# A two-layer conditional attention kernel: the opening in another order, GpSimd's long subtractions in four parts, both probability-value groups side by side

## What is computed

```python
# layer 0: linear attention, 8 heads
q = softmax((xn @ Wq + bq) per head);  k = softmax((xn @ Wk + bk + mask) over the rows)
att = einsum('bnhd,bnhl->bhdl', k, v);  y = einsum('bnhd,bhdl->bnhl', q, att)
# layer 1: softmax attention, 16 heads
att = softmax(einsum('bnhl,bmhl->bnmh', q, k) + mask, axis=2);  y = einsum('bnmh,bmhl->bnhl', att, v)
# both
scale, shift = split(silu(cond) @ W_emb + b_emb)
x = x + silu(ln(y) * (1 + scale) + shift) @ W_out + b_out
```

## Time and profile before

| | before |
|---|---|
| median of 3 runs | 2180.84 us (2180.38 to 2180.98) |
| the profiled execution | 2180.41 us |
| its span, first to last instruction | 2178.6 us |
| TensorE matmuls busy | 2140.4 us, 98% |
| VectorE busy | 1400.7 us, 64% |
| ScalarE busy | 910.7 us, 42% |
| GpSimd busy | 563.9 us, 26% |
| mean granted TensorE clock | 0.995 |

### The profile page before, as it was taken

How to read it: one execution, slowest core, us unless ns; L and a number is a source line. 1 busy time by engine, 2 the same in 40 slices (tenths; PEclk the granted TensorE clock), 3 DMA queues, 4 the chain that set the end, 5 groups by cost and what they waited for, 6 DMA issues and landing times.

```text
span 2178.6 us, 53551 instructions
## 1 busy us (share of the span) xinstructions
PE 2140.4 (98%) x20955; PEld 1859.2 (85%) x20955; DVE 1400.7 (64%) x2986; ACT 910.7 (42%) x2088; POOL 563.9 (26%) x890
## 2 busy tenths in 40 slices
PE   6999999999999999999999999999999999999997
PEld 4888888888888888877888888888888888888886
DVE  6777777777777777766564656565555555555554
ACT  3333333333333333442444444444444444445444
POOL 4233333233333233323222212121212121212120
PEclk9999999999999999999999999999999999999999
DMA  6211000111000111103000000000101010101000
GB/s 207 107 39 39 29 34 34 39 39 39 29 34 34 39 39 39 38 21 117 20 29 29 29 29 30 28 36 22 39 19 39 19 39 19 39 19 39 19 31 21
DMA packets 52165, 86.47 MB, mean 40 GB/s; under 512 B 5667, under 2 KB 14565, under 8 KB 52134
## 3 DMA queue, kind: packets, MB, share of 16 engines
q1 hardware_dynamic: 52118, 86.03, 11.2%
q10 hardware_dynamic: 16, 0.00, 0.0%
HBM read 52.32 MB, written 33.69 MB: 39 GB/s over the span
## 4 chain that ended last, share of the span: by engine, by line
PE 94%; DVE 2%; ACT 1%; issue 1%; DMA 1%; SPq 0%; POOL 0%; DVEq 0%; ACTq 0%
PE bank L537 14%; PE bank L538 13%; PE bank L539 13%; PE bank L546 9%; PE bank L547 8%; PE bank L548 8%; PE bank L1650 5%; PE bank L1676 3%; PE bank L1105 3%; PE bank L1682 3%; PE bank L1693 2%; PE bank L1093 2%; PE bank L1006 1%; PE bank L1616 1%; PE bank L1030 1%; PE bank L1034 1%
## 5 line engine op out<-in xcount | busy, mean ns | idle before, releaser
L546 PE MATMUL bank<-xT_hi,w_hi 128*128 128x256 f32 x1536 | 449.1, 292 | 1.1 <-DVE top L1322 1.1
L547 PE MATMUL bank<-xT_lo,w_hi 128*128 128x256 f32 x1536 | 441.1, 287 | 0.0
L548 PE MATMUL bank<-xT_hi,w_lo 128*128 128x256 f32 x1536 | 437.6, 285 | 0.0
L537 PE MATMUL bank<-w_hi,xT_hi 128*128 128x512 f32 x768 | 316.2, 412 | 4.4 <-DVE bias_all L401 4.4
L546 PEld LDWEIGHTS bank<-xT_hi,w_hi 128*128 128x128 f32 x1536 | 291.3, 190 | 19.9 <-issue 8.9
L539 PE MATMUL bank<-w_lo,xT_hi 128*128 128x512 f32 x768 | 307.1, 400 | 0.0
L538 PE MATMUL bank<-w_hi,xT_lo 128*128 128x512 f32 x768 | 304.0, 396 | 0.0
L547 PEld LDWEIGHTS bank<-xT_lo,w_hi 128*128 128x128 f32 x1536 | 291.8, 190 | 1.5 <-issue 0.2
L548 PEld LDWEIGHTS bank<-xT_hi,w_lo 128*128 128x128 f32 x1536 | 292.4, 190 | 0.0
L537 PE MATMUL bank<-w_hi,h_hi 128*128 128x512 f32 x512 | 217.6, 425 | 5.9 <-DVE h_lo L1364 3.7
L926 ACT ACTIVATE heads<-bank,k_neg 128x128 f32<-128x128 f32 x256 | 70.0, 372 | 358.3 <-DVE k_neg L791 358.3
(11 more groups left out here) (210 smaller groups left out, 4053.6 us busy)
## 6 DMA issues: line engine op xcount, KB each, us to landing
xr<-in_x SPq DMA_DIRECT2D x32, 512.0 KB, 3.4
x_between_layers<-ends SPq DMA_DIRECT2D x64, 256.0 KB, 2.0
xr<-x_between_layers SPq DMA_DIRECT2D x32, 512.0 KB, 3.6
out<-ends SPq DMA_DIRECT2D x64, 256.0 KB, 2.0
store<-in_L_cond_W_emb SPq DMA_DIRECT2D x4, 1024.0 KB, 11.4
mask_rows<-mask_parts SPq DMA_DIRECT2D x128, 2.0 KB
heads<-in_L_cond_emb_w SPq DMA_DIRECT2D x2, 1024.0 KB, 7.2
store<-in_L_cond_emb_w SPq DMA_DIRECT2D x2, 1024.0 KB, 11.5
```

The costliest lines, as they stand in the source:

```text
L537: yield nc.tensor.matmul(bank[:, :], a_hi[:, c, b, :], w_hi[:, m, c, :], start=(c == 0), stop=False)
L546: yield nc.tensor.matmul(dst, w_hi[:, m, c, fs], a_hi[:, c], start=(first and c == 0), stop=False)
L547: yield nc.tensor.matmul(dst, w_hi[:, m, c, fs], a_lo[:, c], start=False, stop=False)
L548: yield nc.tensor.matmul(dst, w_lo[:, m, c, fs], a_hi[:, c], start=False, stop=(last and c == C - 1))
```

## The change

It has three parts.

In the opening, the conditioning vector is loaded behind the key weights, and its tanh, product and transposes move back on all engines, to behind the first half of the projections. The key bias is loaded with the first small loads. ScalarE issues its four mask DMAs ahead of the high part of the key weights, reports each of the four parts of a high part, and copies the key sums behind the turned rows. VectorE normalises the first pair ahead of the low part of the key weights and makes the low part of the value weights behind the query bias. TensorE projects feature groups 0 and 2 of the first keys ahead of the query sums and adds their bias later. GpSimd makes the low part of the output weights in four parts and adds the value bias later.

At the hand-over, GpSimd's `low` goes in four parts, with one report at the end.

In layer 1's loop, `mixed` of both sequences stand side by side, both `turned` are woven into the last two query projections, and VectorE and ScalarE follow: `end_outputs` of both ahead of `end_norm`, `copy_yT` of both ahead of the second half of the queries.

The core of the diff:

```diff
@@ -211,9 +211,9 @@
...
-    loads = [(cond, T["cond_2048"]),
-             (mask_in[:, 0, :], T["mask_BxSx1_fk1"].rearrange("b s o -> b (s o)")),
-             (mask_in[:, 1, :], T["mask_BxS_ff1"])]
+    loads = [(mask_in[:, 0, :], T["mask_BxSx1_fk1"].rearrange("b s o -> b (s o)")),
+             (mask_in[:, 1, :], T["mask_BxS_ff1"]),
+             (m.key_row, T["L0_cond_bk"].rearrange("(o d) -> o d", o=1))]
...
@@ -230,7 +230,8 @@
...
-        sp.dma_start(m.key_row, T["L0_cond_bk"].rearrange("(o d) -> o d", o=1)).then_inc(small_in3, 16)
+            if n == K:
+                sp.dma_start(cond, T["cond_2048"]).then_inc(cond_in, 16)
         for k, name in ((BQ, "L0_cond_bq"), (BV, "L0_cond_bv"), (BO, "L0_cond_b_out")):
             sp.dma_start(m.bias_all[:, k, :], row_everywhere(name)).then_inc(small_in3, 16)
...
@@ -277,21 +278,23 @@
...
-        pool.wait_ge(s["split_hi"], 4)
-        nc.gpsimd.tensor_tensor(m.w_lo[:, O], raw[O], f32(m.w_hi[:, O]), ALU.subtract).then_inc(s["out_lo"], 1)
-        pool.wait_ge(s["out_lo"], 1)
+        pool.wait_ge(s["split_hi"], 4 * C)
+        for c in range(C):
+            nc.gpsimd.tensor_tensor(m.w_lo[:, O, c, :], raw[O][:, c, :], f32(m.w_hi[:, O, c, :]),
+                                    ALU.subtract).then_inc(s["out_lo"], 1)
+        pool.wait_ge(s["out_lo"], C)
+        pool.wait_ge(small_in3, 48)
...
-                    last = nc.scalar.activation(m.w_hi[:, n, c, :], raw[n][:, c, :], ACT.Copy,
-                                                scale=vcol("L0_cond_ln_w", c))
-            last.then_inc(s["split_hi"], 1)
+                    nc.scalar.activation(m.w_hi[:, n, c, :], raw[n][:, c, :], ACT.Copy,
+                                         scale=vcol("L0_cond_ln_w", c)).then_inc(s["split_hi"], 1)
...
@@ -299,20 +302,13 @@
...
-        act.wait_ge(small_in, 16 * len(loads))
-        nc.scalar.activation(cond_tanh, cond, ACT.Tanh, scale=0.5).then_inc(tanh_ready, 1)
...
-        act.wait_ge(vec_ready, 2)
-        high(K)
...
@@ -320,16 +316,23 @@
...
-        part(0)
+        act.wait_ge(vec_ready, 2)
+        high(K)
         for b in range(PAIR):
...
+        part(0)
         high(Q)
+        act.wait_ge(cond_in, 16)
+        nc.scalar.activation(cond_tanh, cond, ACT.Tanh, scale=0.5).then_inc(tanh_ready, 1)
         part(1)
         high(V)
         high(O)
         part(2)
+        act.wait_ge(cond_ps, 1)
+        nc.scalar.activation(m.cond_T[:], ps[6][:, 0:KE * B].rearrange("p (k b) -> p k b", k=KE),
+                             ACT.Copy, scale=0.5).then_inc(cond_ready, 1)
...
@@ -337,16 +340,14 @@
...
-            dve.wait_ge(s["split_hi"], WEIGHTS.index(n) + 1)
             for c in chunks:
+                dve.wait_ge(s["split_hi"], WEIGHTS.index(n) * C + c + 1)
...
-        dve.wait_ge(tanh_ready, 1)
-        nc.vector.scalar_tensor_tensor(cond_tanh, cond_tanh, 1.0, cond, ALU.add, ALU.mult).then_inc(cond_step, 1)
...
@@ -374,17 +375,15 @@
...
-        low(K, (0,))
...
-        low(K, (1, 2, 3))
+        low(K, range(C))
...
-        dve.wait_ge(small_in3, 64)
...
@@ -394,12 +393,16 @@
...
         low(Q, range(C))
-        low(V, range(C))
+        dve.wait_ge(tanh_ready, 1)
+        nc.vector.scalar_tensor_tensor(cond_tanh, cond_tanh, 1.0, cond, ALU.add, ALU.mult).then_inc(cond_step, 1)
         yield
         for k, n in ((1, BQ), (2, BV)):
+            dve.wait_ge(small_in3, 48)
             dve.wait_ge(sum_ps, k + 1)
             nc.vector.tensor_tensor(m.bias_all[:, n, :], ps[SUM_BANKS[k]][:, :], m.bias_all[:, n, :],
                                     ALU.add).then_inc((s["q_bias"], s["bias_v"])[k - 1], 1)
+            if n == BQ:
+                low(V, range(C))
...
@@ -423,10 +426,6 @@
...
-        pe.wait_ge(cond_step, 1)
-        for k in range(KE):
-            last = nc.tensor.transpose(ps[3][:, k * B:(k + 1) * B], cond_tanh[:, k * P:(k + 1) * P], m.ident[0:B, 0:B])
-        last.then_inc(cond_ps, 1)
...
@@ -439,23 +438,28 @@
...
         pe.wait_ge(s["key_bias"], 1)
         total(0)
+        pe.wait_ge(s["split_lo"], 1)
+        yield
         pe.wait_ge(mask_off_ready, 1)
         part(1)
-        pe.wait_ge(s["split_lo"], 1)
-        yield
-
-        pe.wait_ge(cond_ready, 1)
+        yield
         total(1)
         part(2)
+        pe.wait_ge(cond_step, 1)
+        pe.wait_ge(s["xT_lo"], PAIR)
+        for k in range(KE):
+            last = nc.tensor.transpose(ps[6][:, k * B:(k + 1) * B], cond_tanh[:, k * P:(k + 1) * P], m.ident[0:B, 0:B])
+        last.then_inc(cond_ps, 1)
         pe.wait_ge(small_in2, 16 * len(loads2))
         rest = n_vec - 2 * C
         nc.tensor.transpose(ps[7][:, 0:rest], vec_in2, m.ident[0:rest, 0:rest]).then_inc(vec_ps, 1)
+        pe.wait_ge(s["split_lo"], 2)
+        yield
         pe.wait_ge(s["q_bias"], 1)
-        pe.wait_ge(s["split_lo"], 2)
-        yield
         total(2)
         yield
         pe.wait_ge(s["bias_v"], 1)
+        pe.wait_ge(cond_ready, 1)
         pe.wait_ge(s["split_lo"], 3)
         yield
 
@@ -698,13 +702,16 @@
...
-        def biases(pair, slot, first):
-
+        def residual(pair, slot):
             pool.wait_ge(s["xn"], seq(PAIR, pair, PAIR))
             for b in range(PAIR):
                 last = nc.gpsimd.tensor_tensor(xr[:, slot, b], xr[:, slot, b], bias_all[:, BO, :], ALU.add)
             last.then_inc(s["x_biased"], 1)
-            if not first:
+
+        def value_bias(pair, first):
+            if first:
+                pool.wait_ge(s["bias_v"], 1)
...
@@ -723,10 +727,14 @@
...
-            if not first:
+            if first:
+                residual(0, 0)
+                value_bias(0, True)
+            else:
                 low_parts(i - 1)
             if not last:
-                biases(i + 1, (i + 1) % RING, False)
+                residual(i + 1, (i + 1) % RING)
+                value_bias(i + 1, False)
             else:
...
@@ -1036,20 +1044,35 @@
...
-            pe.wait_ge(s["xT_lo"], seq(PAIR, i, PAIR))
-            for f in range(C):
+            def keys(f):
                 dst = ps[f // 2][:, (f % 2) * PAIR * P:(f % 2 + 1) * PAIR * P]
-                if f == 2 and not first:
-                    pe.wait_ge(emb.s["scale"], 1)
                 run(project_features(nc, w_hi, w_lo, K, f, xT_hi, xT_lo, dst, C, True, False))
-                if f == 0:
-                    pe.wait_ge(s["masks_in"], 64 if first else seq(32, i, 32))
-                if f == 0 and first:
-                    pe.wait_ge(s["key_bias"], 2)
+
+            def key_biases(f):
+                dst = ps[f // 2][:, (f % 2) * PAIR * P:(f % 2 + 1) * PAIR * P]
                 done = nc.tensor.matmul(dst, key_bias[:, f * P:(f + 1) * P], mask_rows[:, i % RING, :],
                                         start=False, stop=True)
...
+
+            pe.wait_ge(s["xT_lo"], seq(PAIR, i, PAIR))
+            if first:
+                keys(0)
+                keys(2)
+                next(start)
+                pe.wait_ge(s["masks_in"], 64)
+                pe.wait_ge(s["key_bias"], 2)
+                key_biases(0)
+                key_biases(2)
+            for f in range(C):
+                if first and f % 2 == 0:
+                    continue
+                if f == 2:
+                    pe.wait_ge(emb.s["scale"], 1)
+                keys(f)
+                if f == 0:
+                    pe.wait_ge(s["masks_in"], seq(32, i, 32))
+                key_biases(f)
             if first:
...
@@ -1253,7 +1276,9 @@
...
-            nc.gpsimd.tensor_tensor(w_lo[:, n], m.raw[n], f32(w_hi[:, n]), ALU.subtract).then_inc(s["lo_qk"], 1)
+            for c in range(C):
+                last = nc.gpsimd.tensor_tensor(w_lo[:, n, c, :], m.raw[n][:, c, :], f32(w_hi[:, n, c, :]), ALU.subtract)
+            last.then_inc(s["lo_qk"], 1)
...
@@ -1399,8 +1424,8 @@
...
             if not first:
                 end_outputs(i - 1, 0)
+                end_outputs(i - 1, 1)
                 end_norm(i - 1, 0)
...
@@ -1573,9 +1598,9 @@
...
             if not first:
                 copy_yT(i - 1, 0)
+                copy_yT(i - 1, 1)
             queries_out(i, (2, 3))
             if not first:
-                copy_yT(i - 1, 1)
                 gate(i - 1, 0)
...
@@ -1786,13 +1811,10 @@
...
             if not first:
                 mixed(i - 1, 0, C + 2)
-            run(projected(i, 0, (2,)))
-            woven(projected(i, 0, (3,)), () if first else turned(i - 1, 0))
-            if not first:
                 mixed(i - 1, 1, C + 4)
-            values0 = value_rows(i, 0, first)
-            run(islice(values0, 4))
-            woven(values0, () if first else turned(i - 1, 1))
+            woven(projected(i, 0, (2,)), () if first else turned(i - 1, 0))
+            woven(projected(i, 0, (3,)), () if first else turned(i - 1, 1))
+            run(value_rows(i, 0, first))
             if not first:
...
```

13 lines of the change are left out of this document (4 added, 9 removed).

## The result

The changed kernel takes 2158.4 us (median of 4 runs, 2157.6 to 2159.1), beside 2180.6 us for the kernel before on the same chip: 22.2 us less, ratio 0.9898 with a 95% interval of 0.9881 to 0.9915. I had said 2164, with 2159 to 2171 as the range: the sign and the places were right, the gain came out 5.6 us larger, and the time lies 0.6 us under the range.

The account below looks back on a forecast made before the run. TensorE's matmuls, filling 98% of the span, were taken to bound the kernel. From the profiled 2180.41 us, 2.2 (opening), 5.7 (hand-over) and 8.7 (layer 1's loop) came off: 2163.8, or 2164 against the median, range 2159 to 2171.

Parts of the forecast that it names:

- Hand-over, 5.7: Layer 0 to layer 1: splitting GpSimd's subtraction moves the chain 3.4 us and avoids half rate, 2.3; 5.7 us won.
- Rival B: Hand-over: VectorE gets no turn between GpSimd's four parts, so nothing is gained there; 2170 us, chance 0.06.
- the cited rule: Skill's SBUF page: with two VectorE SBUF inputs and GpSimd reading SBUF, the second to issue fully blocks until the first finishes.
- Opening, 2.2: Kernel's start: earlier value projection and a removed transpose wait, less 2.0 for half rate; 2.2 us won, bounds -1 and +5.5.
- the new wait: Opening: TensorE waits 3.4 us for the value bias before the value projection, with 2.0 us charged for half rate.
- Loop, 8.7: Layer 1's loop, 31 pairs: groups side by side save 0.28 us a pair, 8.7 us; bounds 0 and 9.9.
- 0.09 + 0.09 + 0.10 = 0.28 us a pair: Layer 1's loop: three small losses around one probability-value group, one set of which goes when both groups stand together.
- they cost 0.11 each in either, nothing: Layer 1's loop: weaving transposes into 256-wide instead of 512-wide matmuls changes nothing, 0.11 us each.
- My upper bound of 0.32 a pair: Layer 1's loop: the most that joining the groups was expected to save, 9.9 us over the loop.
- Rival C: Layer 1's loop: the three small losses belong to each group and stay when two stand together; 2173 us, chance 0.08.
- Rival D: Layer 1's loop: z(0) comes too late in each pair, past a 0.9 us margin; slower, 2189 us, chance 0.04.
- Rivals A and E: Opening: A, gains nothing, 2166.5, chance 0.13; E, earlier value bias, no clock fall, 5.5 us, 2161, chance 0.09.

Follow-up runs that it names:

- hand_only: Kernel before the change, with only GpSimd's two hand-over subtractions in four parts each: 5.6 us less than before (ratio 0.9975).
- open_only: Kernel before the change, with the opening's changes alone: 3.3 us less than before (ratio 0.9986).
- loop_only: Kernel before the change, with the change of layer 1's loop alone: 13.2 us less than before (ratio 0.9938).
- three_between: Changed kernel with three 256-wide query matmuls moved between the two probability-value groups: 9.2 us less than before the change (ratio 0.9955), pair 35.90 us.
- second_in_values: Changed kernel with sequence 1's transposes back in the value matmuls and VectorE in its old order: 20.6 us less than before the change (0.9907), pair 35.62.
- weave_ten: Changed kernel with all ten transposes of a pair in the last query chunk: 6.1 us less than before the change, pair 36.03 us.

## Why the prediction was right or wrong

The mechanisms of the forecast held. What failed is the size of one term, the loop of layer 1; the opening added a little.

- **Hand-over, 5.7.** Right in each step: measured 5.6 alone (`hand_only`), one wait of 1.65 us (1.4), full rate behind it. Rival B has fallen: VectorE got its turn between GpSimd's parts. I wrote that the cited rule speaks against the splitting; it doesn't, since it holds for one instruction at a time, and VectorE's step took 1.37 us where it had taken 4.69.
- **Opening, 2.2.** The mechanism was right, the new wait and its half rate included (granted clock 0.54 over the stretch from 40.2 to 43.9). Measured 3.3 by the medians (`open_only`), with an interval from 0.9 to 5. In the profile of the changed kernel it is 1.7: the value bias came 0.8 us later than worked out, and the half rate behind the wait cost 1.65 us (twelve matmuls in 4.45 us, 2.8 at full rate), where I charged 2.0. On the other side I had charged half rate to the first twelve key matmuls, which in the earlier form of the opening run at full rate, 1.6 us more. The sum of 2.2 stands for the later form; the earlier one I had not foreseen.
- **Loop, 8.7.** Here the forecast failed, by 4.5 us (13.2 in `loop_only`). Two terms were mis-sized. First, "0.09 + 0.09 + 0.10 = 0.28 us a pair": the group costs 0.35 (`three_between`). I compared L1682 (0.99) with L1676 (0.90), but L1676 carries 0.02 of its own for being first; inside a run either takes 0.87, so a group pays 0.14 within itself instead of 0.09. Second, "they cost 0.11 each in either, nothing": moving five transposes out of the 512-wide value matmuls gave 0.07 us a pair (`second_in_values`). The steps around one transpose nearly agree (0.316 + 0.027 against 0.23, and 0.202 + 0.028 against 0.12), but summed over the steps that carry them the five cost 0.59 us in the values and 0.55 in the chunk: 0.04 of the 0.07 is found there. The rest is spread over other steps, and why it is so remains open. Together 0.14 x 31 = 4.3 us. My upper bound of 0.32 a pair stood under the true value of 0.43. The loop's 4.5 us alone would give 2159.8, just inside the range; the opening's 1.1 more takes it out.
- **Rival C**, the losses stay with each group, has fallen: with the groups side by side the inner borders step at 0.87. **Rival D**, z(0) late, did not happen: z(0) was ready at 1187.79 and asked for at 1188.75, a margin of 0.96 us where I had worked out 0.9. It was close all the same: `weave_ten` moved the transposes of sequence 0 back by 1.4 us, and 16 of the 22 us were lost.
- **Rivals A and E.** The opening gives something, and the new wait is there with its half rate: both have fallen.
